# Dividing the second attention layer's large matmul blocks over two slots, and reordering the last item of a fused two-layer kernel

## The reference

```
x = x + _L0_attn_ref(_layernorm(x), ...)   # 16 heads of 128, signed softmax, rotary
x = x + _L0_ffn_ref(_layernorm(x), ...)    # 16 experts + 1 shared, top 4
x = x + _L1_attn_ref(_layernorm(x), ...)   # 16 heads of 16, rotary, softmax
x = x + _L1_ffn_ref(_layernorm(x), ...)    # 16 experts + 1 shared, top 4
```

## Time and profile before

| | us |
|---|---|
| median of 3 runs (lowest, highest) | 864.09 (862.94, 867.29) |
| the profiled execution, its own time | 865.04 |
| span of that execution, first to last instruction | 863.3 |
| PE busy in the span | 828.1 (96%) |
| DVE, ACT, POOL busy | 646.3, 525.3, 465.8 |

### The profile page before, as it was taken

How to read it: one execution, slowest core, us unless ns; L and a number is a source line. 1 busy time by engine, 2 the same in 40 slices (tenths; PEclk the granted TensorE clock), 3 DMA queues, 4 the chain that set the end, 5 groups by cost and what they waited for, 6 DMA issues and landing times.

```text
span 863.3 us, 14805 instructions
## 1 busy us (share of the span) xinstructions
PE 828.1 (96%) x4549; PEld 627.4 (73%) x4549; DVE 646.3 (75%) x1350; ACT 525.3 (61%) x1106; POOL 465.8 (54%) x399
## 2 busy tenths in 40 slices
PE   8899999999989999989998999999999999999997
PEld 6678788777878888766887887764444447888886
DVE  5898888999998888998376865868788634676553
ACT  3778788787867888863644533336576554454442
POOL 4565555666665556551666776623300426656774
PEclk9999999999999999999999999999999989999999
DMA  4222222322422223122665357412441132334442
GB/s 157 93 98 87 98 97 97 106 81 87 152 74 99 98 97 110 61 69 60 208 210 182 131 163 275 138 57 73 137 136 51 57 99 93 123 123 142 152 162 65
DMA packets 57426, 99.20 MB, mean 115 GB/s; under 512 B 8272, under 2 KB 19024, under 8 KB 57360
## 3 DMA queue, kind: packets, MB, share of 16 engines
q1 hardware_dynamic: 57360, 98.39, 34.3%
HBM read 71.88 MB, written 9.57 MB: 94 GB/s over the span
## 4 chain that ended last, share of the span: by engine, by line
PE 64%; issue 10%; POOL 10%; DVE 10%; ACT 4%; DMA 2%; SPq 0%; DVEq 0%; POOLq 0%; ACTq 0%
PE ps L974 10%; PE ps L951 10%; PE ps L960 9%; PE ps L319 6%; PE ps L382 5%; PE ps L330 4%; POOL q_sin L526 3%; PE ps L343 3%; PE ps L370 3%; PE ps L1642 2%; PE ps L1523 2%; PE ps L357 2%; PE ps L1612 2%; POOL wqk_lo L513 2%; DVE nm L1834 2%
## 5 line engine op out<-in xcount | busy, mean ns | idle before, releaser
L1098 POOL TENSOR_TENSOR ew_lo<-ew_raw,ew_hi 128x768 fp32r<-128x768 f32 x68 | 128.6, 1892 | 56.7 <-ACT ew_hi L1064 48.5
L1050 ACT ACTIVATE hid_hi<-guw 128x512 fp32r<-128x512 f32 x68 | 43.0, 632 | 156.2 <-POOL guw L1114 106.2
L1153 DVE TENSOR_TENSOR hid_lo<-guw,hid_hi 128x512 fp32r<-128x512 f32 x68 | 78.9, 1160 | 72.4 <-ACT hid_hi L1050 72.3
L1114 POOL TENSOR_TENSOR guw<-gu,cwb 128x512 f32<-128x512 f32 x61 | 80.4, 1318 | 92.4 <-issue 76.4
L526 POOL TENSOR_TENSOR q_sin<-q_sw,sin 128x512 f32<-128x512 f32 x64 | 83.5, 1312 | 51.7 <-DMA q_sw<-q_in 50.4
L1834 DVE TENSOR_REDUCE nm<-ps 128x1 f32<-128x512 f32 x128 | 81.4, 683 | 19.0 <-PE ps L1546 17.8
L1729 ACT ACTIVATE e<-ps 128x512 f32<-128x512 f32 x128 | 68.7, 602 | 35.6 <-PE ps L1642 35.3
L974 PE MATMUL ps<-ew_hi,hid_hi 128*128 128x256 f32 x272 | 78.3, 288 | 2.4 <-DVE hid_lo L1153 1.8
L505 DVE SCALAR_TENSOR_TENSOR w<-ex,rden,sgn 128x512 f32<-128x512 f32 (+3 forms) x128 | 79.0, 680 | 0.0
L433 ACT ACTIVATE ex<-sabs,nmax 128x512 f32<-128x512 f32 (+3 forms) x128 | 61.5, 551 | 28.1 <-DVE nmax L479 28.1
L974 PE MATMUL ps<-ew_lo,hid_hi 128*128 128x256 f32 x272 | 76.8, 282 | 0.0
(11 more groups left out here) (189 smaller groups left out, 2401.6 us busy)
## 6 DMA issues: line engine op xcount, KB each, us to landing
ew_raw<-in_ew SPq DMA_DIRECT2D x68, 384.0 KB, 3.3
q_sw<-q_in SPq DMA_DIRECT2D x128, 128.0 KB, 2.0
cwb<-cw_dram SPq DMA_DIRECT2D x61, 256.0 KB, 3.7
wqk_raw<-in_wqk SPq DMA_DIRECT2D x32, 256.0 KB, 2.6
wv_raw<-in_wv SPq DMA_DIRECT2D x32, 128.0 KB, 2.4
wo_raw<-in_wo SPq DMA_DIRECT2D x32, 128.0 KB, 2.2
qs<-stk_q SPq DMA_DIRECT2D x16, 256.0 KB, 3.5
ks<-stk_k SPq DMA_DIRECT2D x16, 256.0 KB, 4.1
```

The costliest lines, as they stand in the source:

```text
L1098: pool.tensor_tensor(ff[f].ew[1][:, i % EW_SLOTS, :], ew_raw[:, i % RAW_SLOTS, :], fp(ff[f].ew[0][:, i % EW_SLOTS, :]), ALU.subtract).then ...
L1114: pool.tensor_tensor(ff[f].guw[:, i % 2, :], ff[f].gu[:, i % 2, :], ff[f].cwb[:, r % CWB_SLOTS, :], ALU.mult).then_inc(sem("guw"), 1)
L1153: dve.tensor_tensor(ff[f].hid[1][:, i % 2, :], ff[f].guw[:, i % 2, :], fp(ff[f].hid[0][:, i % 2, :]), ALU.subtract).then_inc(sem("hid_lo"), 1)
```

## The change

Four edits, all in the second layer. In `group_pe` and `v_pe` a block is issued in two parts: the first half in the slot that the table names, the second half in the slot behind it (for slot 3 that is slot 0 of the next step), and the DVE operations that read the block move one slot on as well. The output products of steps 19 and 20 stand in slots 1 and 3 instead of behind the step. The last item of the last layer (`ahead`) has its silu multiplied by the route's weight on POOL first, in place, and DVE's product with up then writes `guw`; its first two row tiles raise a semaphore of their own (`y_half`), on which the first of the two last sums waits. POOL makes `ew_low` of expert 0 before the last norm's first half, and those of experts 1 to 4 only after `nm_lo` of the last quad.

```diff
+        def ahead(f, i):
+            return f == 1 and i >= NI - 1
...
+                if (f, i, t) == (1, NI - 1, 1):
+                    last.then_inc(sem("y_half"), 1)
...
+            dst = ff[f].guw
+            if ahead(f, i):
+                silu_done(pool, f, i + 1)
+                dst = ff[f].gu
...
+            if ahead(f, i):
+                wait_f(dve, f, "guw", ROUTED[i])
...
+                if (f, h, k) == (1, 1, 0):
+                    dve.wait_ge(sem("y_half"), 1)
...
-        STEP_Y = {19: (0, 1), 20: (2, 3)}
+        STEP_Y = {(19, 1): 0, (19, 3): 1, (20, 1): 2, (20, 3): 3}
...
-        def group_pe(pe, g, sw):
+        def group_pe(pe, g, sw, part):
...
-            for j in range(3 * DC):
+            for j in range(3 * part, 3 * part + 3):
...
+            if previous(k, j) in STEP_GROUP:
+                group_pe(pe, *STEP_GROUP[previous(k, j)], 1)
             if (k, j) in STEP_GROUP:
-                group_pe(pe, *STEP_GROUP[k, j])
+                group_pe(pe, *STEP_GROUP[k, j], 0)
+            if previous(k, j) in STEP_V:
+                v_pe(pe, STEP_V[previous(k, j)], 1)
             if (k, j) in STEP_V:
-                v_pe(pe, STEP_V[k, j])
+                v_pe(pe, STEP_V[k, j], 0)
+            if (k, j) in STEP_Y:
...
+                y_pe(pe, t, BANK_OF["y", t], 0)
...
+            ew_low(pool, 1, 0)
             ln_pool(pool, 3, (0,))
             ln_xn(pool, 3, 0)
             gw_low(pool, 1)
-            for i in range(3):
-                ew_low(pool, 1, i)
-            for i in range(3, 5):
+            pool.wait_ge(sem("nm_lo"), QUADS)
+            for i in range(1, 5):
                 ew_low(pool, 1, i)
...
-            if (k, j) in STEP_GROUP:
-                group_dve(dve, *STEP_GROUP[k, j])
+            if previous(k, j) in STEP_GROUP:
+                group_dve(dve, *STEP_GROUP[previous(k, j)])
```

More of the change, by code:

```diff
@@ L825, in half_of @@
             return t[:, h * S:(h + 1) * S]
+        def ahead(f, i):
+            return f == 1 and i >= NI - 1
         def ready_f(eng, f, i):
-            if ITEMS[i][0] > 0:
+            if ITEMS[i][0] > 0 and not ahead(f, i):
                 wait_f(eng, f, "guw", ROUTED[i])
@@ L1111, in weighted @@
             wait_f(pool, f, f"cwb_ld{r % CWB_SLOTS}", 16 * ((r - SPREAD[f]) // CWB_SLOTS + 1))
-            wait_f(pool, f, "gu", i + 1)
-            wait_f(pool, f, "hid_lo", i - 1)
-            pool.tensor_tensor(ff[f].guw[:, i % 2, :], ff[f].gu[:, i % 2, :], ff[f].cwb[:, r % CWB_SLOTS, :],
+            dst = ff[f].guw
+            if ahead(f, i):
+                silu_done(pool, f, i + 1)
+                dst = ff[f].gu
+            else:
+                wait_f(pool, f, "gu", i + 1)
+                wait_f(pool, f, "hid_lo", i - 1)
+            pool.tensor_tensor(dst[:, i % 2, :], ff[f].gu[:, i % 2, :], ff[f].cwb[:, r % CWB_SLOTS, :],
                                ALU.mult).then_inc(sem("guw"), 1)
@@ L1141, in gated @@
             dst = ff[f].gu
-            if ITEMS[i][0] == 0:
+            if ITEMS[i][0] == 0 or ahead(f, i):
                 wait_f(dve, f, "hid_lo", i - 1)
                 dst = ff[f].guw
+            if ahead(f, i):
+                wait_f(dve, f, "guw", ROUTED[i])
             if i < TANH_ITEMS[f]:
@@ L1340, in build_program, with previous @@
         TAIL_ZT, TAIL_ZC, TAIL_Y = 5, 6, 7
+        def previous(k, j):
+            return (k, j - 1) if j else (k - 1, HEADS - 1)
         def tile_at(n):
@@ L1383, in step @@
                     order.append(("v", STEP_V[k, j]))
+                if (k, j) in STEP_Y:
+                    order.append(("y", STEP_Y[k, j]))
             for i in range(ROW_T, NI + 1):
@@ L1511, in a1_sp @@
             maxima(sp, 7)
-        def group_pe(pe, g, sw):
+        def group_pe(pe, g, sw, part):
             t, mt, h = GROUPS1[g]
-            bank_wait(pe, "qk", 2 * g + sw)
-            if sw == 0:
+            if part == 0:
+                bank_wait(pe, "qk", 2 * g + sw)
+            if sw == 0 and part == 0:
                 pe.wait_ge(sem("xT_lo"), 2 * DC * 2 + DC * (h + 1))
                 pe.wait_ge(sem("w1_lo"), 2 * t + 2)
-            if g == 0:
+            if g == 0 and part == 0:
                 wait_f(pe, 0, "gu", PAIR_UNTIL)
-            for j in range(3 * DC):
+            for j in range(3 * part, 3 * part + 3):
                 ch, (pw, px) = j // 3, PARTS[j % 3]
@@ L1524, in group_pe, with v_pe @@
                                  half_of((xT_hi, xT_lo)[px][:, ch, :], h), start=j == 0, stop=j == 3 * DC - 1)
[L1525 to L1536, removed]
+            if part == 1:
+                last.then_inc(sem("qk1_ps"), 1)
+        def v_pe(pe, v, t2):
+            if t2 == 0:
+                bank_wait(pe, "v", v)
+                pe.wait_ge(sem("w1_lo"), 5)
+            t = 2 * v + t2
+            for j in range(3 * DC):
+                ch, (pw, px) = j // 3, PARTS[j % 3]
+                last = pe.matmul(ps[:, BANK_OF["v", v], t2 * D:(t2 + 1) * D], (xT_hi, xT_lo)[px][:, ch, t * P:(t + 1) * P],
+                                 w1[pw][:, 4, ch, :], start=j == 0, stop=j == 3 * DC - 1)
+            if t2 == 1:
+                last.then_inc(sem("v1_ps"), 1)
         def maximum_pe(pe, n):
@@ L1589, in a1_row_pe @@
                 for g, sw in ROW_GROUP.get(i, ()):
-                    group_pe(pe, g, sw)
+                    for half in range(2):
+                        group_pe(pe, g, sw, half)
                 if i in ROW_V:
-                    v_pe(pe, ROW_V[i])
+                    for half in range(2):
+                        v_pe(pe, ROW_V[i], half)
             if i in ROW_LEAD:
```

40 lines of the change are left out of this document (20 added, 20 removed).

## The result

| us | before | changed |
|---|---|---|
| median, executions | 866.3 (15) | 872.65 (15) |
| lowest, highest | 862.0, 875.4 | 865.8, 881.86 |
| profiled execution, its span | 865.04, 863.3 | 872.65, 870.9 |

The ratio is 1.0069, with a 95% interval of 1.0041 to 1.0096: slower by 6.0 us (3.6 to 8.3). I had forecast 3.5. A second set of 12 executions of the changed kernel gave 1.0068 (1.0035 to 1.0102).

What follows compares the result with a forecast made beforehand. The prediction took PE, busy 96% of the span, as the bound. It summed +5.08 us through the output products, -0.8 for the last norm and -0.75 for the tail to +3.5: 864.09 became 867.6 us, range 860.8 to 872.

Steps and rivals of the forecast that it cites:

- the likeliest case: Whole kernel: no change, within about 0.5% of the time before, chance 0.52.
- The divisions and the chain: Second attention: divided blocks cost 0.20 or 0.39 us each and delay `qk_hi`, stopping PE; +5.33 us at step 14.
- The stops and the clock: Before steps 7 and 12: PE waits for late exps, 1.16 us at step 7; no half clock behind them in the sum.
- rival 1: Behind PE's new stops: a further half-clock stretch, +3.3 us, 870.9 us; with two, 874 us; chance 0.25.
- The output products: Steps 19 and 20: extra divisions against a filled 0.61 us wait, net +0.17 to -0.61, taken as -0.25 us.
- The last norm: Before the logits: POOL kept still until `nm_lo`, so `nm_s` is quicker and the logits start earlier; -0.8 us.
- The tail: After the last silu: POOL weights first and the first sum starts earlier; -0.75 us, bounds -0.65 and -0.85.
- The early weighting: Last item: POOL's product before DVE's, so `hid_hi` can start 0.0 to 0.2 us earlier.
- The base: Starting time of the forecast: the kernel before at a median of 864.09 us.
- Rival 2: Second attention: no stops and nearly free divisions, so only the gains count; -2.4 us, 861.7 us, chance 0.14.
- rival 4: Whole kernel: divisions nearly free and the clock's fall behind 696 us absent; 858.5 us, chance 0.05.
- Rival 3: Behind 696 us: the clock's fall doesn't recur; 3.3 us less than forecast, 864.3 us, chance 0.14.

Runs made afterwards that it cites:

- stops filled: The changed kernel plus four 128x512 matmuls nobody reads on PE ahead of the first scores of step 7 and of step 12; 870.45 us, ratio 1.0017 to before.
- whole blocks: The changed kernel with all blocks of groups 4 to 7 and both v blocks in one piece again, other edits kept; 862.49 us, ratio 0.9956 to before.
- division alone: The kernel before with only the blocks of groups 4 to 7 and the v blocks divided; 877.51 us, ratio 1.0109 to before.
- norm undone: The changed kernel with undivided blocks and POOL's old order round the last norm; profile only: `nm_s` 4.27 us, PE waiting 2.4 us for it.

## Why the prediction was wrong

The sign and the places were right, the sum at full clock was close, and the likeliest case was the wrong one.

- **The divisions and the chain**: +5.33 predicted at step 14, 5.7 measured with the stops filled. `qk_hi` of group 5 started 2.98 us later (2.9 predicted), the half lasts 0.89 (603.36 to 604.25), and PE waited 1.01 before step 7 for 1.16 predicted. For group 7 it was 5.4 at full clock (stops filled) against 4.9. The divisions account for the loss at full clock: it goes with them (whole blocks), and 3.8 of it with the two in front of the stops. The step that I left out is small: the transposes of step 10 also waited 0.3 for `rc`, as those of step 5 for `rs`.
- **The stops and the clock, rival 1**: this is the step that failed: the sum put nothing for falls behind its own two stops. I wrote that waits of 0.6 us had left the clock at 1.00 and gave a fall behind a stop 0.25. Behind the two stops the two profiles of the changed kernel show falls 3 times of 4, with filled stops 0 of 2. Four places are few; that the stops cost clock rests as much on the mean clock, 0.988 with them and 0.993 with them filled. The wait of 0.6 us was no safe bound either: the longest falls, from 573 on, follow one of 0.48. And I had read the clock of the kernel before as 1.00 up to 696.1, though its profile has a fall at 242 to 246 as well. The profiled execution of the changed kernel had a fall behind both stops; for two I had 874, it took 872.65, and my range ended at 872.0, so it left out a case that I had priced. My price for two falls was 6.6 us; together they cost 3.3, since the first lasts 3.5 us where I had taken 6.7, and half of its 1.45 us is paid back by `ks`.
- **The output products**: -0.25 predicted, -0.05 measured. 0.65 was won by 662.35 and 0.6 lost at step 21, where the transposes' bank waits for the new `y_add`. I had read the order of PE, not what the ring of banks makes of it.
- **The last norm**: -0.8 predicted, -0.7 against the same profile. But one profile showed the cheap case of an unstable wait; in two others the old order costs over 3 us more, about half of it waiting for `nm_s`, the rest the fall behind it. That the changed kernel would have lost more without it is likely and not shown: division alone, which lacks this gain and the tail's too, stands 9.5 us above the kernel before (ratio 1.0109).
- **The tail**: -0.75 predicted, -0.75 measured (8.35 us late at the last silu, 7.6 at the span's end): 0.6 by the end of the second sum, and the rest between there and the end of the span. The early weighting gave the 0.0 at the low end of its 0.0 to 0.2. The Trainium skill's rule in "SBUF — State Buffer", "Who interferes with whom", would start POOL only behind `hid_lo`, which ends at 862.43; it starts at 862.33 and keeps its 1.29 us, so the rule is neither needed nor clearly shown here. At `nm_s` the trace agrees with that rule in that DVE is held: with the norm undone the small operation ends at 681.20 (676.93 + 4.27) and POOL's last low part at 681.17 (675.81 + 5.36). It was held for more than one instruction of POOL's, which the rule does not say.
- **The base**: I started from 864.09, a median of three; 15 executions give 866.3. Of the 5.05 us between 867.6 and 872.65 that is 2.2, and without it the measurement would lie inside my range: that three executions came out low was bad luck, and resting on three was the fault. The clock is 2.6 more: the changed kernel's mean is 0.0038 lower, at 6.9 us for a hundredth (1.9 us if the means take in every execution). At equal clock the change cost 0.8 less than the 3.5 forecast, and about 1 us is left, within the uncertainty of the medians.

Rival 2 (divisions free) is refuted by 5.7 us, and rival 4 with it. Rival 3 is not refuted: the fall in step 28 came in the first profile of the changed kernel (705 to 712) and not in the second, so it was never a property of the change. Without falls the terms give 5.7 - 0.05 - 0.7 - 0.75 = 4.2 us against the first profile of before and, with 1.7 us more waiting for `nm_s` in its second, 2.5 against that; the line has +2.7 ± 0.7.

## What to carry to other kernels

Before a block is divided, ask which copy or read-out on another engine stands in a fixed place and waits for the block's end, and count the matmuls that are left between that end and the first that needs the engine. Where PE will stand still for a microsecond, count a stretch at half clock as likely, not as a rival; filling the wait with idle matmuls is a cheap test of it. Compare kernels by many executions and with the mean granted clock beside the time: a base of three was 2.2 us off here. A wait seen once in one profile has no price yet: where two engines meet by chance, look at a second execution.

## What the runs showed of the hardware

- Where TensorE falls to 1.2 GHz differs between executions of one program. Two profiles of the kernel before share no such place in front of the last matmul; whole executions had a mean clock of 1.00 (the best 860.37 us with whole blocks) or 0.98 (871.24).
- Many falls came behind short waits: behind the two stops 3 of 4, behind waits of 2.1 and 2.4 us for `nm_s` 2 of 2, in step 28 with its waits of 0.9 and 0.6 us 5 of 11, and where the experiments filled the wait with matmuls 0 of 4. That filling keeps the clock up is not shown by this alone, since the longest falls (573 to 597, 4 of 13) stand among idle matmuls that all the kernels have. The Trainium skill, "TensorE: Matmul & The Clock Gate", "Part 1: The HAM clock gate", speaks of an idle engine in front of a fall. The trace agrees only in direction: in 606.70 to 608.40 PE was busy 0.73 of 1.70 us, not idle throughout.
- Two DVE operations of 128x16, 0.17 us each alone, take 0.73 and 1.73, 2.51 and 1.72, or 4.27 (the first alone) when POOL makes `ew_lo` beside them.
